# Two slots of 16 pairs in place of three, with unread products in TensorE's idle time: a matmul with layer norm on one core

## The reference

```python
keep = (u >= 0.1).astype(x.dtype)
x_drop = x * keep / (1.0 - 0.1)
y = x + jnp.matmul(adj, x_drop)
m = jnp.mean(y, axis=-1, keepdims=True)
v = jnp.var(y, axis=-1, keepdims=True)
return (y - m) / jnp.sqrt(v + 1e-5)
```

## Time and profile before

| | before |
|---|---|
| median of 3 runs | 642.63 us |
| the profiled execution | 642.77 us |
| its span, first to last instruction | 640.9 us |
| outside the span | 1.9 us |
| DMA | 274.83 MB, mean 429 GB/s |
| PE (matmul) busy | 516.3 us, 81% of the span |
| TensorE's mean granted clock | 0.918 of full |
| loads of `adj` blocks | 44 whole slots, 12 parts |

### The profile page before, as it was taken

How to read it: one execution, slowest core, us unless ns; L and a number is a source line. 1 busy time by engine, 2 the same in 40 slices (tenths; PEclk the granted TensorE clock), 3 DMA queues, 4 the chain that set the end, 5 groups by cost and what they waited for, 6 DMA issues and landing times.

```text
span 640.9 us, 5635 instructions
## 1 busy us (share of the span) xinstructions
PE 516.3 (81%) x2308; PEld 176.5 (28%) x2308; DVE 52.1 (8%) x231; ACT 10.8 (2%) x18; POOL 18.0 (3%) x27
## 2 busy tenths in 40 slices
PE   0397797887977886897879869787887879879996
PEld 0122222232322322232222223222222223223325
DVE  5100101000010100001010010100001010010102
ACT  0000000000000000000000000000000000000000
POOL 0000000000000000000000000000000000000000
PEclk9997997988989899897989898898998889898999
DMA  9999999999999999999999999999999999999998
GB/s 383 424 448 432 429 430 443 413 440 426 439 428 450 421 441 437 433 427 443 413 440 429 430 432 449 424 441 435 431 431 439 414 443 428 429 429 431 429 424 347
DMA packets 9794, 274.83 MB, mean 429 GB/s; under 512 B 1216, under 2 KB 1472, under 8 KB 2496
## 3 DMA queue, kind: packets, MB, share of 16 engines
q1 hardware_dynamic: 9504, 274.63, 99.5%
q10 hardware_dynamic: 288, 0.16, 0.1%
HBM read 272.66 MB, written 2.13 MB: 429 GB/s over the span
## 4 chain that ended last, share of the span: by engine, by line
DMA 70%; PE 27%; issue 1%; SPq 0%; DVE 0%; POOL 0%; POOLq 0%; ACT 0%; DVEq 0%
DMA raw<-adj_dram 70%; PE acc L170 27%; SPq L131 0%; PE turned L190 0%; POOL rstd L275 0%; DVE stats L245 0%; POOLq L46 0%; ACT sums L216 0%; DVE rows L241 0%; SPq L135 0%; SPq L134 0%; DVE moments L250 0%; POOLq L280 0%; DVE final_normed L268 0%; DVE var_eps L253 0%
## 5 line engine op out<-in xcount | busy, mean ns | idle before, releaser
L170 PE MATMUL acc<-raw,dropped 128*64 128x504 f32 x2048 | 490.5, 639 | 91.4 <-POOLq L280 90.0
L170 PEld LDWEIGHTS acc<-raw,dropped 128*64 128x64 f32 x2048 | 153.3, 148 | 416.7 <-issue 294.0
L241 DVE TENSOR_TENSOR rows<-turned,x_sb 126x256 f32<-126x256 f32 x16 | 6.8, 424 | 544.4 <-PE turned L190 544.4
L275 POOL TENSOR_TENSOR rstd<-var_eps,minus_half 126x4 f32<-126x4 f32 x16 | 16.2, 1011 | 613.2 <-DMA raw<-adj_dram 328.3
L190 PE MATMUL turned<-join,sums 128*126 128x64 f32 x128 | 17.5, 279 | 10.9 <-ACT sums L216 10.9
L190 PEld LDWEIGHTS turned<-join,sums 128*126 128x126 f32 x128 | 15.3, 189 | 24.8 <-ACT sums L216 24.8
L216 ACT COPY sums<-acc 128x504 f32<-128x504 f32 x16 | 9.2, 578 | 616.1 <-PE acc L170 616.1
L256 DVE TENSOR_SCALAR normed<-rows,moments,rstd 126x64 f32 x64 | 15.7, 309 | 26.7 <-POOL rstd L275 26.7
L180 PE MATMUL final_turned<-x_sb,eye 128*128 128x64 f32 x2 | 0.7, 448 | 17.9 <-DVE dropped L235 17.9
L245 DVE BATCH_NORM_STATS2 stats<-rows 126x6 f32<-126x64 f32 x64 | 9.7, 214 | 0.5
L170 PE MATMUL final_acc<-raw,dropped 128*64 128x128 f32 x124 | 7.1, 275 | 0.0
(11 more groups left out here) (17 smaller groups left out, 3.5 us busy)
## 6 DMA issues: line engine op xcount, KB each, us to landing
raw<-adj_dram SPq DMA_DIRECT2D x30, 5544.0 KB, 26.8
raw<-adj_dram SPq DMA_DIRECT2D x14, 5040.0 KB, 29.2
raw<-adj_dram SPq DMA_DIRECT2D x2, 3024.0 KB, 21.3
raw<-adj_dram SPq DMA_DIRECT2D x2, 2520.0 KB, 26.9
raw<-adj_dram SPq DMA_DIRECT2D x2, 2016.0 KB, 21.3
raw<-adj_dram SPq DMA_DIRECT2D x2, 1512.0 KB, 24.6
x_sb<-x_dram SPq DMA_DIRECT2D x1, 2080.0 KB, 12.1
dropped<-u_dram SPq DMA_DIRECT2D x1, 2048.0 KB, 7.6
```

The lines of the kernel that those rows point to most:

```text
L170: last = nc.tensor.matmul(sum_bank[t * D:(t + 1) * D, 0:width], dropped[:, t * PAIRS + q, :], raw[:, s, start:start + width], start=(q == ...
L241: nc.vector.tensor_tensor(rows[:, :, :], turned[0:ROWS, 0:GROUPS, :], x_sb[0:ROWS, bass.ds(b * GROUPS, GROUPS), :], ALU.add).then_inc(turn ...
L275: nc.gpsimd.tensor_tensor(rstd[:, :], var_eps[:, :], minus_half[0:ROWS, :], ALU.pow).then_inc(rstd_ready, 1)
```

## The change

`raw` has two slots of 16 pairs in place of three of 11, 11 and 10. The parts of the last block are 8, 8, 6, 4, 3, 2 and 1 pairs. Block 0's first slot comes in two parts, and block 14's second slot in two loads of 10 and 6 pairs (`JOINED`). TensorE gets a new operation, `keep_busy`: one float32 matmul of 128 weight columns and 504 moving columns out of `dropped` into a PSUM bank `spare` that nobody reads. It runs in two loops of its own in each block: at the top of the block three times, and behind the first slot four times. In blocks 14 and 15 (`last_two` is 1) each loop runs once. So there are 14 x 7 + 2 x 2 = 102 such matmuls in all.

```diff
--- before.py
+++ after.py
@@ -19,14 +19,20 @@
 
 
 
-SLOT_PAIRS = [(0, 11), (11, 22), (22, 32)]
+SLOT_PAIRS = [(0, 16), (16, 32)]
 SLOTS = len(SLOT_PAIRS)
 SLOT = max(q1 - q0 for q0, q1 in SLOT_PAIRS) * PAIR
-PARTS = [(0, 0, 6), (0, 6, 11), (1, 11, 17), (1, 17, 22), (2, 22, 26), (2, 26, 29), (2, 29, 31), (2, 31, 32)]
+PARTS = [(0, 0, 8), (0, 8, 16), (1, 16, 22), (1, 22, 26), (1, 26, 29), (1, 29, 31), (1, 31, 32)]
+JOINED = [(2, 4), (4, 7)]
 IN_SLOT = [sum(part[0] == s for part in PARTS) for s in range(SLOTS)]
 
 
 FINAL = [(0, 8), (8, 16), (16, 22), (22, 26), (26, 29), (29, 31), (31, 32)]
+MORE_TOP, MORE_SLOT = 2, 3
 
 
 
@@ -79,6 +85,7 @@
         turned = psum("turned", [P, 512 // D, D])
         final_acc = psum("final_acc", [P, 512])
         final_turned = psum("final_turned", [P, 512])
+        spare = psum("spare", [P, 512])
 
         x_loaded = semaphore("x_loaded")
         u_loaded = semaphore("u_loaded")
@@ -120,11 +127,11 @@
 
         @block.sync
         def _(sp):
-            def load_part(b, n):
-                s, q0, q1 = PARTS[n]
+            def load_parts(b, n0, n1):
+                s, q0, q1 = PARTS[n0][0], PARTS[n0][1], PARTS[n1 - 1][2]
                 q_slot = SLOT_PAIRS[s][0]
                 sp.dma_start(raw[:, s, (q0 - q_slot) * PAIR:(q1 - q_slot) * PAIR],
-                             adj[b, :, q0 * PAIR:q1 * PAIR]).then_inc(part_loaded[n], DMA)
+                             adj[b, :, q0 * PAIR:q1 * PAIR]).then_inc(part_loaded[n0], DMA)
 
             def load_slot(b, s):
                 q0, q1 = SLOT_PAIRS[s]
@@ -133,23 +140,22 @@
 
             sp.dma_start(dropped[:, :, :], u_dram).then_inc(u_loaded, DMA)
             sp.dma_start(x_sb[:, :, :], x).then_inc(x_loaded, DMA)
-            for s in range(SLOTS):
-                load_slot(0, s)
+            for n in range(IN_SLOT[0]):
+                load_parts(0, n, n + 1)
+            load_slot(0, 1)
             with sp.Fori(1, BLOCKS - 2) as b:
                 for s in range(SLOTS):
                     sp.wait_ge(multiplied, (b - 1) * SLOTS + s + 1)
                     load_slot(b, s)
-            for s in range(SLOTS - 1):
-                sp.wait_ge(multiplied, (BLOCKS - 3) * SLOTS + s + 1)
-                load_slot(BLOCKS - 2, s)
-            sp.wait_ge(multiplied, (BLOCKS - 2) * SLOTS)
-            for n, (s, q0, q1) in enumerate(PARTS):
-                if s == SLOTS - 1:
-                    load_part(BLOCKS - 2, n)
+            sp.wait_ge(multiplied, (BLOCKS - 3) * SLOTS + 1)
+            load_slot(BLOCKS - 2, 0)
+            sp.wait_ge(multiplied, (BLOCKS - 3) * SLOTS + 2)
+            for n0, n1 in JOINED:
+                load_parts(BLOCKS - 2, n0, n1)
             for n, (s, q0, q1) in enumerate(PARTS):
                 if q0 == SLOT_PAIRS[s][0]:
                     sp.wait_ge(multiplied, (BLOCKS - 2) * SLOTS + s + 1)
-                load_part(BLOCKS - 1, n)
+                load_parts(BLOCKS - 1, n, n + 1)
 
             sp.wait_ge(multiplied, (BLOCKS - 1) * SLOTS + 1)
             pair = TILES * P
@@ -163,6 +169,10 @@
 
         @block.tensor
         def _(pe):
+            def keep_busy():
+                nc.tensor.matmul(spare[:, 0:WIDTH], dropped[:, 0:TILES, :],
+                                 dropped[:, :, :].rearrange("p c d -> p (c d)")[:, 0:WIDTH], start=True, stop=True)
             def multiply(sum_bank, width, s, q_slot, q0, q1, pairs):
                 for q in range(q0, q1):
                     for t in range(TILES):
@@ -179,11 +189,17 @@
 
             nc.tensor.matmul(final_turned[:, 0:D], eye[:, :], x_sb[:, CHUNKS, :], start=True, stop=False)
             with pe.Fori(0, BLOCKS) as b:
+                last_two = (b + 2) >> 4
+                with pe.Fori(0, 1 + MORE_TOP - MORE_TOP * last_two):
+                    keep_busy()
                 for n, (s, q0, q1) in enumerate(PARTS):
                     pe.wait_ge(landed, b * len(PARTS) + n + 1)
                     last = multiply(acc, WIDTH, s, SLOT_PAIRS[s][0], q0, q1, PAIRS)
                     if q1 == SLOT_PAIRS[s][1]:
                         last.then_inc(multiplied, 1)
+                        if s == 0:
+                            with pe.Fori(0, 1 + MORE_SLOT - MORE_SLOT * last_two):
+                                keep_busy()
                 pe.wait_ge(sums_ready, b + 1)
 
                 for i in range(GROUPS):
@@ -276,12 +292,13 @@
                                         ALU.pow).then_inc(rstd_ready, 1)
 
             def pass_slot(b, s):
-                pool.wait_ge(raw_loaded[s], b * DMA + DMA)
+                pool.wait_ge(raw_loaded[s], b * DMA if s == 0 else b * DMA + DMA)
                 pool.sem_inc(landed, IN_SLOT[s])
 
-            def pass_part(n, loads):
-                pool.wait_ge(part_loaded[n], loads * DMA)
-                pool.sem_inc(landed, 1)
+            def pass_parts(n0, n1, loads):
+                pool.wait_ge(part_loaded[n0], loads * DMA)
+                pool.sem_inc(landed, n1 - n0)
 
             nc.gpsimd.memset(minus_half[:, :], -0.5).then_inc(minus_half_ready, 1)
             nc.gpsimd.memset(eye[:, :], 0.0).then_inc(squares_zeroed, 1)
@@ -296,19 +313,17 @@
                                     base=-D, pattern=[[-1, D]], channel_multiplier=1).then_inc(join_ready, 1)
 
             pool.wait_ge(minus_half_ready, 1)
-            pass_slot(0, 0)
+            for n in range(IN_SLOT[0]):
+                pass_parts(n, n + 1, 1)
             with pool.Fori(0, BLOCKS - 2) as b:
-                for s in range(1, SLOTS):
-                    pass_slot(b, s)
+                pass_slot(b, 1)
                 pass_slot(b + 1, 0)
                 rsqrt(b)
-            for s in range(1, SLOTS - 1):
-                pass_slot(BLOCKS - 2, s)
+            for n0, n1 in JOINED:
+                pass_parts(n0, n1, 1)
             for n, (s, q0, q1) in enumerate(PARTS):
-                if s == SLOTS - 1:
-                    pass_part(n, 1)
-            for n, (s, q0, q1) in enumerate(PARTS):
-                pass_part(n, 2 if s == SLOTS - 1 else 1)
+                pass_parts(n, n + 1, 2 if s == 0 or any(n == n0 for n0, n1 in JOINED) else 1)
                 if n == 1:
                     rsqrt(BLOCKS - 2)
             rsqrt(BLOCKS - 1)
```

## The result

The changed kernel takes **644.38 us** (median of 15 runs, 642.93 to 645.07) against 642.57 (15 runs, 642.36 to 643.00): a ratio of 1.0024, 95% interval 1.0016 to 1.0032. It is slower by 1.8 us, just beyond the 0.2% that the prediction took as the limit of what can be told. The forecast of 643.1 lay 1.3 us low; the measured time lies inside the stated range of 641.9 to 645.0. The profiled execution took 643.98, its span is 642.0.

The account below looks back on a forecast made before the run. DMA bandwidth was taken to set the pace, with the end of the program TensorE's. Loop 0, fewer pieces -0.2 and the end +0.7 summed to +0.5 us on 642.63: 643.1 us, range 641.9 to 645.0.

Parts of the forecast that it names:

- The sum's 0 for the loop: In the block loop: unread products cost 0, covered by DMA, as no reload waits for them and the clock stays high.
- The latency of 2.7 us: At each reload: time a load needs beyond its transfer, at most 2.7 us, part of it after the last byte.
- Rival 1: At the end of each 16-pair multiply: the reload comes too late, 0.6 us in each of 28 slots, 660 us; 8%.
- 2.3 us of cover are left: At each reload in the loop: 5.0 us of cover less 2.7 of latency leaves 2.3 us at full clock.
- the term for the end, 0.7 us: In block 15: the one product left behind the second 8-pair part delays the next matmuls and the end by 0.7 us.
- the start: At block 0: the first slot comes in two parts, so its reload has more cover; no size given.
- Rival 2: In the last block: products of 1.23 us or a low clock delay the end, up to 644.5 us; 6%.
- Narrow loops: In the small product loops: each of 32 causes an instruction fetch on one DMA engine, 19 us, 662 us; 4%.
- Larger loads: In the blocks' loads: larger loads run some 0.4% faster, worth 2.4 us, 640.7 us; 5%.
- - 0.2: In the last two blocks' loads: 9 pieces in place of 12, worth -0.2 us.

Follow-up runs that it names:

- experiment 2: The changed kernel with the first slot's reload released by the fourth product behind its multiply, not by the multiply's last matmul: 679.66 us (the run e6_late_reload).
- experiment 1: The changed kernel with two slots and no unread products at all: 657.93 us (the run e2_none).
- e6_late_reload: The changed kernel with the first slot's reload released by the fourth product behind its multiply, not by the multiply's last matmul: 679.66 us, ratio to before 1.0592.
- e2_none: The changed kernel with two slots and no unread products at all: 657.93 us, ratio to before 1.0210.
- e9_start_too: e4_top14 with 13 products instead of 4 behind block 0's first slot: 642.53 us, ratio to before 1.0000.
- e4_top14: The changed kernel with three products kept at the top of block 14, the count there dropping in block 15 only: 643.36 us, ratio to before 1.0012.
- after_again1: The changed kernel itself, unedited, run again for another trace: 644.31 us in that trace.
- experiment 5: The changed kernel with its block loop split, three products ahead of block 14 and none behind that: 643.59 us (the run e5_none_at_end).
- experiment 7: Two more traces of the changed kernel, 644.31 and 643.17 us, and e4_top14 with 13 products behind block 0's first slot, 642.53 us.
- e5_none_at_end: The changed kernel with its block loop split, three products ahead of block 14 and none behind that: 643.59 us, ratio to before 1.0016.

## Why the prediction was right and where it was off

**Right: DMA sets the pace, and two slots keep it.** The block's step is 38.10 us, the multiply 13.74, the idle times 0.95 and 1.72. The sum's 0 for the loop holds from the third slot on. In the profiled execution the loads weren't late at all: block 14's first slot landed at 567.06, where the kernel before, reckoned back by 6 pairs from its landing at 574.64, had 574.64 - 3024 / 423 = 567.5 (an estimate).

**Right in mechanism: the cover.** The latency of 2.7 us, taken as the dear end, is 2.5 by measure (experiment 2). Rival 1, the late reload, had a price of 0.6 us for 28 slots and 660 us. Without products the kernel takes 657.9. That the two figures are so close is in part luck: single holes were larger than 0.6 us, and not every slot had one. The forecast had the products keep that cover, and they do; it was my expectation for experiment 1, written later, that doubted it and fell. One figure of the prediction was too kind: "2.3 us of cover are left" takes it that a hole opens only when the cover is below the latency. The traces show holes earlier:

| cover, issue of the reload to the landing ahead of it | hole behind it |
|---|---|
| -0.2 us (`e6_late_reload`) | 2.7 |
| 1.4 and 1.5 (`e6_late_reload`, at full clock) | 1.3 and 1.6 |
| 2.2 to 4.0 (`e2_none`) | none to 1.8 |
| 3.3 (`e9_start_too`) | none |
| 3.5 (`e4_top14`) | 0.9 |
| 3.9 (`after_again1`) | 1.2 |
| 4.6 to 5.0 (the three traces of the changed kernel) | none |

A hole here is what the step between two landings has beyond 19.05 us. In `e2_none` steps behind a hole are longer too (0.5 us once at a cover of 4.8), so its row mixes the two.

So of the 5.0 us of cover at full clock not 2.3 were surely to spare but about 1. Why holes begin above the latency is not shown.

**Off: the term for the end, 0.7 us.** It said: "Let X be the landing of block 15's second part of 8 pairs. TensorE ends it at X + 0.1 + 9.52 - 3 x 0.85 = X + 7.1." That assumes that TensorE waits for X. It doesn't: it has been behind since 567.15. X was at 605.5, where GpSimd's wait for that part ends:

```profile
605.56 1.01 POOL L291 TENSOR_TENSOR rstd<-var_eps,minus_half 126x4 f32<-126x4 f32 x1 [37.24 <-DMA raw<-adj_dram]
```

By the prediction's own sum the loads alone let TensorE end block 15 at X + 7.25 + 13.6 = 626.4. The last piece (504 KB) fits that: it was issued at 598.9 and landed 25.8 us later, at 624.7.

```profile
raw<-adj_dram SPq DMA_DIRECT2D x1, 504.0 KB, 25.8
```

TensorE's own work for the two blocks, without products and at full clock, is 29.0 + 27.3 = 56.3 us by the rows of experiment 5, so it would have been done at 623.4 and had 2.9 us to spare. The three products take 3.2 of them, which passes the slack by 0.3. The slow multiply at block 14's top (15.15 in place of 13.74) adds 1.4. TensorE was done at 628.1: **1.7 us** late in place of 0.7. So the sum's 0.7 for one product was near right for a wrong reason: three products less 2.9 us of slack come to 0.3 us. What the sum lacked altogether is the low clock at the top of block 14, which follows from the change itself: one product there leaves 2.64 us idle, where three leave 0.95.

**Off: the start.** "At block 0 the first slot comes in two parts, so its reload has more cover" is true of the first slot. The second is multiplied behind 6.9 to 8.5 us of idle time, in 15.1 to 16.1 us, and its reload's cover (4.6 to 3.9 us) decides whether a hole of about 1 us opens. One of the three traces has it. With this place and block 14's top mended the median is that of the kernel before (experiment 7). Rival 2 named the low clock as a mishap of the last block at 6%, with "the last blocks are dense" as the reason against. In block 14 it is the rule: all three traces have it.

**The other rivals.** Narrow loops didn't fetch: two packets, as before. Only `e5_none_at_end`, with a longer program, had a third. Larger loads do not run faster by the 0.4% I had left open: 38.12 to 38.10 is 0.05%. On the Trainium skill's fixed cost of about 2 us per DMA ("DMA: Bandwidth & Descriptors", Anatomy of one DMA; stated there for loads issued by GpSimd, where these are SyncE's) the runs show both sides: 2.5 us where a load starts on idle engines, and 0.02 to 0.13 us for one load more in a block where they are queued behind one another (38.10, 38.12 and 38.25 us for two, three and four).

**Chances.** I gave 20% to slower by over 0.2%; it came out at 0.24%, while three quarters had gone to no change. With the two terms above the sum would have been 642.63 - 0.2 + 1.7 and up to 1 of the start, 644.1 to 645.1.

## What to carry to other kernels

With a ring of slots, reckon the cover, the time between a reload's issue and the last landing ahead of it, at the slowest multiply that occurs and not at the usual one: here 4.6 to 5.0 us held, and with 4 us or less a late load, an idle engine and a low clock fed one another until 15 to 37 us were gone. Four small slots gave the cover back in the same memory for 2 us, three slots (one pair more of memory) cost nothing. And at the end of a program look for the point from which the engine no longer waits, and for the slack that the loads leave behind it (2.9 us here): what is added beyond that slack counts in full, and the point may lie a whole block ahead of where the loads are cut fine.

## What the runs showed that was not expected

- Behind `turned` and a run of products of 126 columns the granted clock was 0.66 in a window with PE busy for 3.77 of 4.00 us. In the changed kernel, with three of 504 columns in the same place, the multiply behind them took 13.74 us.
- A load of 8064 KB takes 2.5 us longer from issue to landing when nothing is queued ahead of it (21.55 against 19.05).
- The cost of cutting a block of 16,128 KB into more queued loads is small and not even: 38.10, 38.12, 38.25 us for two, three and four.
- At block 14's top two products more gain 1 us: in the three traces of the changed kernel an idle time of 2.64 us was followed by a slow multiply, and in the traces with 0.95 there by none. The idle time alone doesn't decide it: in `e6_late_reload` the multiply behind 2.56 us took 13.74, and the one behind 2.53 us 15.44.
- The last store of 32 KB took 1.4 to 2.4 us from issue to landing, which is 1 us of the program's time.
